# Cross-attention in a decoder layer: the low halves of the exponentials move from VectorE to GpSimd, each behind the next group's mask

## What is computed

```python
scores = jnp.einsum('bhqd,bhkd->bhqk', qh, kh) * inv_sqrt_d
scores = jnp.where(causal, scores, jnp.finfo(scores.dtype).min)
attn = jax.nn.softmax(scores, axis=-1)
out = jnp.einsum('bhqk,bhkd->bhqd', attn, vh)
```

## Time and profile before

| what | value |
|---|---|
| median of 3 runs | 2077.9 us (2069.17 to 2090.64) |
| the profiled execution: its own time | 2056.93 us |
| its span | 2055.2 us, granted clock of TensorE 0.993 |
| PE busy | 1993.3 us, 97% of the span |
| DVE busy | 1645.9 us, 80% |
| ACT busy | 1028.8 us, 50% |
| POOL busy | 722.5 us, 35% |

### The profile page before, as it was taken

How to read it: one execution, slowest core, us unless ns; L and a number is a source line. 1 busy time by engine, 2 the same in 40 slices (tenths; PEclk the granted TensorE clock), 3 DMA queues, 4 the chain that set the end, 5 groups by cost and what they waited for, 6 DMA issues and landing times.

```text
span 2055.2 us, 46172 instructions
## 1 busy us (share of the span) xinstructions
PE 1993.3 (97%) x16976; PEld 1228.0 (60%) x16976; DVE 1645.9 (80%) x3682; ACT 1028.8 (50%) x1569; POOL 722.5 (35%) x709
## 2 busy tenths in 40 slices
PE   8999999999999999999999987999999999998998
PEld 3666666676676666666667654455555555554553
DVE  5557988888888898898888888858888888877867
ACT  5425434444453553544445354536565665555545
POOL 1003223323323322332332321535555454544533
PEclk9999999999999999999999998999999999999999
DMA  6801011011011001101101122489999999998948
GB/s 227 79 24 45 13 54 54 0 54 54 10 44 54 23 30 54 54 0 54 54 4 50 43 89 78 152 230 280 292 297 288 299 296 293 287 278 270 284 87 327
DMA packets 134324, 267.24 MB, mean 130 GB/s; under 512 B 32699, under 2 KB 42939, under 8 KB 134236
## 3 DMA queue, kind: packets, MB, share of 16 engines
q1 hardware_dynamic: 110108, 226.06, 33.9%
q0 software_dynamic: 24128, 40.01, 10.0%
HBM read 208.67 MB, written 57.42 MB: 129 GB/s over the span
## 4 chain that ended last, share of the span: by engine, by line
PE 78%; DVE 11%; DMA 6%; issue 3%; ACT 1%; POOL 1%; DVEq 0%; POOLq 0%; ACTq 0%
PE ring L915 34%; PE moe_bank L1705 20%; PE ring L975 6%; DVE quad L1294 6%; DMA expert_sums<-tion_then_expert_weights,scatter_index 4%; PE moe_bank L1774 4%; PE fold L483 3%; PE quad L1030 2%; DVE maxima L1294 2%; PE ring L1047 2%; PE ring L982 1%; PE moe_bank L1740 1%; PE ring L1055 1%; DMA expert_sums<-tion_then_expert_weights 1%; PE moe_bank L1752 1%
## 5 line engine op out<-in xcount | busy, mean ns | idle before, releaser
L178 POOL DMA_INDIRECT slot_table<-table_records,slot_of_choice x204 | 202.9, 994 | 482.3 <-PE ring L915 327.7
L915 PE MATMUL ring<-xT_split,tion_then_expert_weights 128*128 128x256 f16 x2304 | 267.2, 273 | 0.0
L915 PE MATMUL ring<-tion_then_expert_weights,xT_split 128*128 128x512 f16 x1152 | 259.9, 379 | 0.0
L915 PEld LDWEIGHTS ring<-xT_split,tion_then_expert_weights 128*128 128x128 f16 x2304 | 221.9, 98 | 36.8 <-issue 7.9
L1154 ACT ACTIVATE scratch<-ring 128x512 f16<-128x512 f32 x224 | 130.5, 595 | 199.8 <-PE ring L915 199.5
L885 POOL TENSOR_SCALAR_AFFINE_SELECT scratch<-scratch 128x1024 f32<-128x1024 f32 x64 | 70.3, 1099 | 379.1 <-ACT scratch L1174 376.3
L1654 POOL DMA_INDIRECT expert_sums<-tion_then_expert_weights,scatter_index x64 | 125.7, 1965 | 193.2 <-DMA expert_sums<-tion_then_expert_weights,scatter_index 58.6
L915 PEld LDWEIGHTS ring<-tion_then_expert_weights,xT_split 128*128 128x128 f16 x1152 | 109.0, 98 | 131.9 <-issue 7.9
L1294 DVE CUSTOM_DVE_ANT_0 quad<-quad,causal_penalty 128x128 f32<-128x128 f32 (+1 forms) x512 | 164.8, 394 | 13.8 <-PE quad L1013 10.7
L1255 DVE SCALAR_TENSOR_TENSOR scratch<-ring,scratch 128x512 f16<-128x512 f32 x192 | 129.1, 684 | 44.3 <-ACT scratch L1154 44.3
L1705 PE MATMUL moe_bank<-w_down_split,hidden_T_split 128*128 128x512 f16 x576 | 136.2, 382 | 5.8 <-DVE hidden_T_split L1921 5.8
(11 more groups left out here) (246 smaller groups left out, 4015.7 us busy)
## 6 DMA issues: line engine op xcount, KB each, us to landing
gate_up_landing<-in_w_gate SPq DMA_DIRECT2D x43, 704.0 KB, 5.7
gate_up_landing<-in_w_up SPq DMA_DIRECT2D x43, 704.0 KB, 5.9
scratch<-in_w_down SPq DMA_DIRECT2D x43, 512.0 KB, 4.8
scratch<-in_w_gate SPq DMA_DIRECT2D x21, 704.0 KB, 5.6
scratch<-in_w_up SPq DMA_DIRECT2D x21, 704.0 KB, 5.8
tion_then_expert_weights<-in_w_down SPq DMA_DIRECT2D x21, 512.0 KB, 4.9
scratch<-in_w_down SPq DMA_DIRECT2D x43, 192.0 KB, 6.3
xT_in<-in_xT SPq DMA_DIRECT2D x16, 512.0 KB, 4.4
```

The source lines that it names most:

```text
L178: pool.indirect_dma_start(self.dram, bass.IndirectOffsetOnAxis(ap=self.slot[:, tb, c:c + 1], axis=0), self.record[:, tb, c, :], None, boun ...
L915: last = pe.matmul(out_, left(a, c), right(b, c), start=(n == 0 and not onto), stop=(n == 3 * chunks - 1))
```

## The change

Step P on DVE (L1304 before) is taken out of the three DVE lists and out of DVE's code. The same subtraction is written in POOL's code, with the same wait for the high half and the same signal `pready`, and it stands in both POOL lists: the order is MASK 0, MASK 1, P 0, MASK 2, P 1, MASK 3, P 2, P 3, so that each group's subtraction comes behind the next group's mask.

```diff
 POOL_BODY = [
     ("XS", 0, 0), ("CS", 0, 0),
 ] + SCATTERS + [
-    ("MASK", 0, 0), ("MASK", 1, 0), ("MASK", 2, 0), ("MASK", 3, 0),
+    ("MASK", 0, 0), ("MASK", 1, 0), ("P", 0, 0), ("MASK", 2, 0), ("P", 1, 0), ("MASK", 3, 0), ("P", 2, 0), ("P", 3, 0),
 ]
...
+                elif name == "P":
+                    pool.wait_ge(phigh, b.n(0, 4, 0, g + 1))
+                    own_wait(pool, taken)
+                    pool.tensor_tensor(ps[:, g % 2, 1, :, :], p32[:, g % 2, :, :], ps[:, g % 2, 0, :, :],
+                                       ALU.subtract).then_inc(pready, 1)
...
-                elif name == "P":
-                    dve.wait_ge(phigh, b.n(0, 4, 0, g + 1))
-                    dve.tensor_tensor(ps[:, g % 2, 1, :, :], p32[:, g % 2, :, :], ps[:, g % 2, 0, :, :],
-                                      ALU.subtract).then_inc(pready, 1)
```

## The result

| | before | after |
|---|---|---|
| median of 3 runs | 2077.9 us (2069.17 to 2090.64) | 2205.2 us (2194.75 to 2214.72) |
| profiled execution: own time, span | 2056.93, 2055.2 us | 2214.72, 2213.0 us |
| granted clock of TensorE in it | 0.993 | 0.964 |
| PE busy | 1993.3 us, 97% | 2053.2 us, 93% |
| DVE busy | 1645.9 us, 80% | 1575.6 us, 71% |

The change makes the kernel 6.1% slower: the ratio is 1.061, with a 95% interval of 1.052 to 1.071. The prediction was 2202 us, in a range of 2152 to 2228. In the kernel after, a line behind POOL's new code has a number 5 higher than before, and one behind the place where DVE's step was has a number 1 higher: L1174 became L1179, L1310 became L1311.

What follows compares the result with a forecast made beforehand. PE, busy 97%, was taken as the bound, so lateness costs in full. Stalls 86 us, body 16 4 us and clock 34 us sum to 124, which on the median 2077.9 gives 2202 us; range 2152 to 2228.

Steps and rivals of the forecast that it cites:

- What bounds the kernel: In a body PE has no room: whatever comes late for it lengthens the body in full; at most 12.5 us could be won.
- Price on POOL: One subtraction of 1536 columns on POOL takes 3.10 us, between 2.13 and 3.20; on DVE it took 1.83.
- P 0: The first subtraction, behind MASK 1 on POOL, makes PE stand still for 2.62 us ahead of AV 0.
- P 2: The subtraction behind MASK 3 on POOL gives PE a second stall, 3.09 us, ahead of AV 2.
- P 1, P 3, XS at nothing: The other two subtractions and POOL's XS end before PE wants them and cost nothing; XS has 9 us of cover.
- The stalls together: Both stalls come to 5.71 us a body, 86 us over 15 bodies.
- The clock: PE's clock falls behind 3 of 4 stalls in bodies 1 to 15, at 1.5 us each: 34 us, between 0 and 51.
- Body 16: In the last body, where PE already waits for two DVE subtractions, 4 us are added, between nothing and 8.
- No falls of the clock: Rival, chance 0.25: PE has the stalls but its clock holds; 2168 us.
- Smaller stalls: Rival, chance 0.03: POOL's subtraction takes 2.13 us, the stalls are 3.8 us a body; 2137 us, more with the clock.
- More waiting between POOL and DVE: Rival, chance 0.1: POOL waits for DVE, so P 0 or P 2 starts up to 0.87 us later; 2215 to 2228 us.
- Not slower: Rival, chance 0.02: each subtraction ends on POOL before PE needs it; at best 2065 us.

Runs made afterwards that it cites:

- E9: E8 with the subtractions of body 16 back on DVE; 2064.2 us, 1.001 of the kernel before.
- E6: The changed kernel with each subtraction split: POOL takes heads 0 and 1, DVE heads 2 and 3 at its old place; 2105.5 us, 1.015 of the kernel before.
- E3: The changed kernel with only P 2 put ahead of MASK 3 in POOL's order; 2129.5 us, 1.027 of the kernel before.
- E2: The changed kernel with only P 0 put ahead of MASK 1 in POOL's order; 2186.2 us, 1.050 of the kernel before.
- E1: The changed kernel with P 0 put ahead of MASK 1 and P 2 ahead of MASK 3 on POOL; 2096.2 us, 1.010 of the kernel before.
- E7: E5 with the subtractions of body 16 back on DVE; 2126.9 us, 1.024 of the kernel before.
- E8: E1 with DVE's scan RS moved behind O 0, where no subtraction is left; 2069.3 us, 1.005 of the kernel before.
- E4: The changed kernel with overwritten PE matmuls ahead of the waits of AV 0 and AV 2 in bodies 1 to 15; 2148.6 us, 1.035 of the kernel before.
- E5: E1 with DVE's scan RS moved behind Y 2,1 and S2 1; 2142.0 us, 1.031 of the kernel before.

## Why the prediction was right, and where it was off

- **What bounds the kernel: right.** PE has no room in a body, and whatever is late for it costs in full. E9 fits: with 110 us of work taken off DVE, 35 of them off its busy time, the time is within 0.1%.
- **Price on POOL: right.** 3.10 us was forecast, 3.092 is the mean of 64 and 3.277 the longest. The straight line through 256 and 1024 columns holds beyond them, and at 768 too: 0.673 + 512 x 0.00190 = 1.65, measured 1.66. The estimate of 3.37 us by the Trainium skill (GPSIMD Engine Reference, 3.1 Elementwise) was 9% too high here, and the measurement decides.
- **P 0: right, 0.12 too much.** 2.50 us for 2.62. MASK 1 ends at 329.38 and PE is ready at 332.54 - 2.50 = 330.04: a cover of 0.66 us where the rows of before gave 0.58.
- **P 2: right, 0.17 too much.** 2.92 us for 3.09. MASK 3 ends at 344.65 and PE is ready at 344.94. The cover is 0.29 and not 0.11, and of that the hand-over took back 0.07 (0.17 for 0.1).
- **P 1, P 3, XS at nothing: right.** AV 1 and AV 3 have no wait in their rows, and no product of the next body waits for POOL.
- **The stalls together:** 81 us for 86.
- **The clock: the step that was mis-sized.** 34 us was forecast, from 22.5 falls at 1.5 us. There were 27 falls, the first stall of all 15 bodies and the second of 12. Five of them lasted 6.8 us instead of 3.4, in the same five bodies that have the wait ahead of OUT. That is 32 times 3.4 us at half speed, 1.7 us each, less the 3.7 us that fell into the second stalls: 51 us, or 1.6 each. So the 1.5 a piece was nearly right and the number was wrong, 32 for 22.5. The forecast's own upper end, 51, was met. The choice of 3 in 4 lay between a stretch with 1.8 us of idle time that kept the clock and one with 1.31 and 0.99 that lost it. The stalls of 1.10 and 1.42 us in E6 kept it every time. Those of 2.50 us lost it 15 times of 15 here, but 11 of 15 in E3; those of 2.92 us 12 times here and 14 in E2. So the length of a stall doesn't decide it alone, and what else does isn't shown.
- **Body 16: right, with luck.** 5.3 us for 4, but the 4 was picked between nothing and 8. PE waits there 3.58, 1.04 and 2.23 us for POOL in place of 1.31 and 0.99 for DVE, 4.6 us more.
- **What was not forecast:** the waits ahead of OUT, 3.5 us; the tail, 5.2 us; the experts' stage, 11.3 us. In the tail PE stands 4.15 us ahead of the router's product, at 1447.61, and the clock reads 0.50 over the next 4 us; before it didn't stand there. The profile names nobody for it: ACT waits 2.94 us before the copy ahead of it, for a reason that it doesn't show either. PE stands at this place, 1.9 to 2.6 us in its longest piece, in the traces of E1 to E7 too, also in E7, where body 16 has the subtractions on DVE as before; it doesn't in those of E8 and E9. So the place of the subtractions alone doesn't bring it. In the experts' stage the clock falls at 1852, 1907 and 2030 us where it fell only at 1874 before. No experiment was made for either. The change doesn't touch the experts' stage, and over all the traces that stage takes 743 to 760 us, so chance is possible; this stays open.
- **The median agrees better than the parts.** The profiled executions differ by 158 us, 34 more than forecast, and the medians by 127. The 136 us of the bodies are read from one trace on each side, the profiled execution of before lay 21 us under its median and that of after 9 above its own. The clock's shortfall of 17 us and the 20 us that weren't forecast are made up for by this, so that 2202 came so close to 2205 is in part luck. How much, three runs on each side can't tell.
- **The rivals.** "No falls of the clock" would have given 2168, or 2165 from the kernel before on E4's chip; E4, which has just that case, took 2148.6. "Smaller stalls" fell with the price, 3.09 us and not 2.13. "More waiting between POOL and DVE" was wrong for this order: DVE does wait, its pair of products takes 2.58 us beside P 0 in place of 0.87, but nobody waits for DVE there:

```profile
330.54 2.58 DVE L1274 SCALAR_TENSOR_TENSOR weights_split<-exp_scores,score_rows,weights_split 128x256 f16<-128x256 f32 x2
```

It was the right mechanism for the other orders, and worth 24 us in E1. The longer pairs are 26 us in all and so part of why DVE's busy time fell by 70 us and not by the 117 of the removed work, against "by over 100" in the prediction. "Not slower" was wrong at this place, but E1 shows that in bodies 1 to 15 its condition, each subtraction ready before PE needs it, can be met by POOL's order alone.

## What to carry to other kernels

When work moves to an engine that is idle most of the time, its share of busy time says nothing; what counts is what stands ahead of the moved step in that engine's queue, and by how much the duration exceeds the time from there to the consumer. Take that time from the trace for each place, and look at what else becomes late when the place is changed: here the better place for P 0 stood beside DVE's scan and held it up. And relief of an engine that nobody waits for is worth nothing. Here it was even smaller than the work removed, since most of the 110 us came back as waiting inside DVE's other instructions.

## What the runs showed of the hardware that was not expected

- A stall in PE's work can cost more than its length. Beside stalls of 2.50 us the clock fell to 1.2 GHz for 3.4 us in 15 of 15 bodies of the kernel after and in 11 of 15 of E3. Beside those of 2.92 us it fell in 12 of 15 (five times for 6.8 us) and in 14 of 15 of E2, and beside those of 2.06 us in 6 of 14 of E5 and 8 of 14 of E7. Stalls of 1.10 and 1.42 us had no fall in 30 (E6). Filling the stalls with matmuls kept the clock at 1.00 in bodies 1 to 15 and saved 54 us (E4).
- Waiting for the other engine is inside an instruction's duration in the profile and counts as busy: DVE's conversion of 12 columns read 1.97 us for 0.17, its sum of 128 columns 2.41 for 0.28, a pair of 256 columns 4.51 for 0.88. No row of the view of waits names this time; what shows it is an instruction many times its usual length that ends just behind one of POOL's.
- POOL's subtraction of an f16 from an f32 to an f16 costs about 1.90 ns a column and 0.2 us ahead, from its times at 256, 768, 1024 and 1536 columns (0.67, 1.66, 2.13 and 3.09 us).
